# Second attention fed from on-chip q, k and v, and another order of scores within a slot

## The reference

```
x = x + ga * attn0(layernorm(x) * (1 + ca) + sa)     # layer 0: 16 heads of 16, 4096 given keys and values
x = x + gb * ffn0(layernorm(x) * (1 + cb) + sb)      # 8 experts, top 2, bfloat16 products
x = x + ga' * attn1(layernorm(x) * (1 + ca') + sa')  # layer 1: 16 heads of 16, k and v from the same 1024 tokens
x = x + gb' * ffn1(layernorm(x) * (1 + cb') + sb')   # a causal attention with 16 heads of 128, then 16 experts, top 6
```

## Time and profile before

| what | value |
|---|---|
| three timed runs | 2124.57, 2126.62, 2134.29 us; median 2126.62 us |
| profiled execution | 2117.84 us, span of its trace 2116.0 us |
| PE / DVE / ACT / POOL busy | 1746.9 / 1427.0 / 1085.5 / 526.8 us |
| mean granted TensorE clock | 0.889 of full |
| attention 0, first to last second score | about 105 to 771 us |
| attention 1, block begins, first pass begins, last sums taken | 946, 956, 1270 us |
| share of attention 0 and 1 in the page's costliest rows | first pass maxima on DVE 757.7 us, exponentials on ACT 668.8 us |

### The profile page before, as it was taken

The page is one execution under the profiler, slowest core; times in us unless marked ns, Lnnn a source line. Parts: engine busy times, 40 slices in busy tenths (PEclk is TensorE's granted clock), DMA queues, the critical chain, the costliest instruction groups (busy, mean ns, idle before and its releaser), DMA issues. The chain is left out here.

```text
span 2116.0 us, 28258 instructions
## 1 busy us (share of the span) xinstructions
PE 1746.9 (83%) x9835; PEld 1051.8 (50%) x9836; DVE 1427.0 (67%) x1894; ACT 1085.5 (51%) x2169; POOL 526.8 (25%) x541
## 2 busy tenths in 40 slices
PE   3599999999999983445468891599999999859997
PEld 3144343343434323232123331488888888748886
DVE  5589999999999934624346763666666666656665
ACT  1078777777877771222235670345455544424432
POOL 3323432343234101213233311211111111002223
PEclk7599999999999995675768995699999999959998
DMA  3211111111111022133112213100000000023432
GB/s 105 49 50 40 44 53 50 43 43 52 47 48 38 16 90 66 41 119 65 51 49 72 68 66 98 39 14 20 20 8 20 20 12 10 1 52 114 120 106 65
DMA packets 54448, 110.17 MB, mean 52 GB/s; under 512 B 8761, under 2 KB 23097, under 8 KB 52819
## 3 DMA queue, kind: packets, MB, share of 16 engines
q1 hardware_dynamic: 52835, 106.07, 17.3%
q10 hardware_dynamic: 1520, 2.88, 0.5%
HBM read 79.33 MB, written 23.31 MB: 49 GB/s over the span
## 5 line engine op out<-in xcount | busy, mean ns | idle before, releaser
L393 DVE TENSOR_REDUCE a_max_part<-psum 128x1 f32<-128x1024 f32 x640 | 757.7, 1220 | 186.1 <-PE psum L296 180.7
L443 ACT ACTIVATE a_probs<-psum 128x512 f32<-128x512 f32 x1280 | 668.8, 604 | 200.3 <-PE psum L347 198.9
L347 PE MATMUL psum<-a_q_max,a_k_rows 51*128 51x512 f32 x1280 | 456.1, 494 | 8.7 <-ACT a_probs L443 7.3
L347 PEld LDWEIGHTS psum<-a_q_max,a_k_rows 51*128 51x128 f32 x1280 | 183.7, 192 | 406.7 <-ACT a_probs L443 308.8
L336 PE MATMUL psum<-a_probs,a_v_ext 128*32 128x512 f32 x2560 | 359.0, 635 | 0.0
L296 PE MATMUL psum<-a_k_rows,a_q_rows 48*128 48x512 f32 x1280 | 317.0, 449 | 49.3 <-DMA a_q_rows<-q 23.8
L296 PEld LDWEIGHTS psum<-a_k_rows,a_q_rows 48*128 48x128 f32 x1280 | 150.6, 201 | 85.7 <-DVE a_max_part L393 33.5
L168 POOL TENSOR_TENSOR a_k_rows<-a_k_in,a_k_rows 16x2048 fp32r<-16x2048 f32 (+1 forms) x64 | 187.3, 2926 | 4.9
L1518 PE MATMUL psum<-high_t_parts,high_gu 128*128 128x512 f32 x600 | 146.5, 395 | 6.8 <-DVE high_t_parts L1612 6.8
L254 POOL TENSOR_TENSOR a_max_bf<-a_neg_max,a_zeros 128x8 bf16<-128x8 f32 x64 | 14.5, 227 | 488.7 <-issue 470.1
L1223 PE MATMUL psum<-wide_k_t,wide_q_t 128*128 128x512 f32 (+3 forms) x576 | 131.2, 355 | 1.7 <-DVE wide_id_bf L1422 1.7
(11 more groups left out here) (175 smaller groups left out, 2056.4 us busy)
## 6 DMA issues: line engine op xcount, KB each, us to landing
o<-a_o_out SPq DMA_DIRECT2D x64, 256.0 KB, 2.0
a_k_in<-in_k SPq DMA_DIRECT2D x32, 256.0 KB
gu_in<-in_w_gu SPq DMA_DIRECT2D x25, 256.0 KB, 2.9
a_q_rows<-q SPq DMA_DIRECT2D x32, 192.0 KB, 3.5
high_cw<-cw SPq DMA_DIRECT2D x24, 256.0 KB, 3.9
a_k_in<-in_k SPq DMA_DIRECT2D x32, 128.0 KB
a_v_in<-in_v SPq DMA_DIRECT2D x16, 256.0 KB, 12.7
a_q_rows<-q_high SPq DMA_DIRECT2D x64, 64.0 KB, 2.4
```

What stands on the lines that cost most here:

```text
L347: pe.matmul(psum[:, self.bank_of(self.filling(j)), :], k_rows[rows, b, k0:k0 + P], self.q_max[rows, u % 2, :], start=True, stop=True).then ...
L393: dve.tensor_reduce(self.max_part[:, u % 2, c // self.nch, c % self.nch:c % self.nch + 1], psum[:, 2 * (n % 2):2 * (n % 2) + 2, :], AX.XY, ...
L443: act.activation(self.probs[:, p % self.pring, :], psum[:, self.bank_of(self.filling(j)), :], ACT.Exp).then_inc(self.exp_done, 1)
```

## The change

**Attention 1 without DRAM.** `project` for layer 1 makes high and low parts of k as well as of q (`highs`, `lows`), in the order q, k of the first eight heads, then q, k of the others, and leaves v in `v_sb` in SBUF. The tensors q1, k1, v1, their stores and the loads of k and v are gone, and so is `split_keys` in attention 1; `copy_v` reads `v_sb`. The attention's tiles are now there during `project`, whose block clears them on POOL (`prepare`). `load_q` for attention 1 is twelve DMAs a head, SBUF to SBUF: per strip three of q (16 partitions by 1,024) and three of k (16 partitions by 512).

**Who issues, and when.** For head 0, in both attentions, SP issues strip 0 and ACT strip 1. Only heads 0 to 2 are loaded before the first unit; in attention 1 heads 3 to 5 now follow one per unit, and later heads as their buffers come free.

**Clears.** `q_rows`, `max_bf` and `v_ext` are cleared by POOL in the block ahead (`clear`) instead of by DVE at the start of the attention's own block; in attention 0 that is in setup.

**Slot order.** Second score j, pair `one` (strip 1, then 0), second score j+1, the turning of the maxima where the slot has it, pair `two` (strip 0, then 1), second scores j+2 and j+3, products.

The core of the diff:

```diff
+def send_rows(eng, strips, rows, sources, h, per_strip, loaded):
+    at = HD * (h % 8)
+    for n in strips:
+        cols = slice(0, T) if per_strip is None else slice(n * per_strip, (n + 1) * per_strip)
+        for m, src in enumerate(sources):
+            row = STRIP * n + HD * m
+            eng.dma_start(rows[row:row + HD, :].bitcast(F32), src[at:at + HD, h // 8, cols].bitcast(F32)).then_inc(loaded, 16)
...
+    def prepare(self, block):
+        @block.gpsimd
+        def _(pool):
+            pool.memset(self.zeros[:, :], 0.0).then_inc(self.zeros_ready, 1)
+            pool.memset(self.k_rows[:, :, :].bitcast(F32), 1.0).then_inc(self.k_set, 1)
+            self.clear(pool)
...
-            load_q(sp, q_rows[:, 0, :], 0, self.q_loaded[0])
-            for h in range(1, nb):
-                load_q(sp, q_rows[:, h, :], h, self.q_loaded[h])
-            for h in range(1, self.early + 1):
-                sp.wait_ge(self.k_split, 2 * h)
-                self.load_k(sp, h)
-                sp.wait_ge(self.v_ready, h)
-                self.load_v(sp, h)
+            load_q(sp, (0,), q_rows[:, 0, :], k_rows[:, 0, :], 0, self.q_loaded[0])
+            for h in range(1, first_heads):
+                load_q(sp, (0, 1), q_rows[:, h, :], k_rows[:, h, :], h, self.q_loaded[h])
+            got = first_heads
...
-                if half == 1 and h + nb < H:
-                    load_q(sp, q_rows[:, h % nb, :], h + nb, self.q_loaded[h % nb])
+                if got < min(H, nb + (u + 1) // 2):
+                    load_q(sp, (0, 1), q_rows[:, got % nb, :], k_rows[:, got % nb, :], got, self.q_loaded[got % nb])
+                    got += 1
...
                 second_wait(u, j)
-                second_wait(u, j + 1)
                 second_chunk(u, j)
-                second_chunk(u, j + 1)
                 if one < self.chunks:
                     first_wait(one)
-                    first_half(one, 0)
-                    first_half(one, 1).then_inc(self.s1_full, 1)
+                    first_half(one, 1)
+                    first_half(one, 0).then_inc(self.s1_full, 1)
+                second_wait(u, j + 1)
+                second_chunk(u, j + 1)
                 if j + 2 == self.turn_at and u + 1 < us:
                     turn_maxima(u + 1)
-                second_wait(u, j + 2)
-                second_chunk(u, j + 2)
                 if two < self.chunks:
                     first_wait(two)
-                    first_half(two, 1)
-                    first_half(two, 0).then_inc(self.s1_full, 1)
-                second_wait(u, j + 3)
-                second_chunk(u, j + 3)
+                    first_half(two, 0)
+                    first_half(two, 1).then_inc(self.s1_full, 1)
+                for n in (j + 2, j + 3):
+                    second_wait(u, n)
+                    second_chunk(u, n)
...
+            act.wait_ge(self.q_set, 1)
+            if not raw:
+                act.wait_ge(self.k_set, 1)
+            load_q(act, (1,), q_rows[:, 0, :], k_rows[:, 0, :], 0, self.q_loaded[0])
             put_row(0)
...
-                attention = Attention(nc, core, psum, ident, ident_bf, "a1", T // P, 6, k1, v1, o1)
+                attention = Attention(nc, core, psum, ident, ident_bf, "a1", T // P, 6, o1, v_sb=v_sb)
```

More of the change, by code:

```diff
@@ L677, in _, with project @@
             act.wait_ge(taken, 4)
-def project(nc, psum, tag, h_t, w, names, q_high, q_low, q_out=None, k_out=None, v_out=None):
+def project(nc, psum, tag, h_t, w, names, highs, lows, v_sb=None, attention=None):
     with ExitStack() as ctx:
         r = Room(nc, ctx, tag, CLEARED)
-        k_sb = r.sb("k", [P, DC, T]) if k_out is not None else None
-        v_sb = r.sb("v", [P, H, TT, HD]) if v_out is not None else None
-        full, high_done, low_done, k_taken = r.sem("full"), r.sem("high_done"), r.sem("low_done"), r.sem("k_taken")
-        v_full, v_taken, stored = r.sem("v_full"), r.sem("v_taken"), r.sem("stored")
+        full, high_done, low_done = r.sem("full"), r.sem("high_done"), r.sem("low_done")
+        v_full, v_taken = r.sem("v_full"), r.sem("v_taken")
         block = r.block()
-        pieces = [(i, c, half) for i in range(1 if k_out is None else 2) for c in range(DC) for half in range(2)]
-        if q_out is not None:
-            @block.sync
-            def _(sp):
-                heads = P // HD
-                for c in range(DC):
-                    sp.wait_ge(high_done, 2 * c + 2)
-                    sp.wait_ge(low_done, 2 * c + 2)
-                    for at, src in ((0, q_high), (HD, q_low), (2 * HD, q_high)):
-                        sp.dma_start(q_out[heads * c:heads * (c + 1), at:at + HD, :], src[:, c, :].bitcast(F32)).then_inc(stored, 16)
-                for c in range(DC):
-                    sp.wait_ge(k_taken, 2 * c + 2)
-                    sp.dma_start(k_out[c * P:(c + 1) * P, :], k_sb[:, c, :]).then_inc(stored, 16)
-                sp.wait_ge(v_taken, TT)
-                sp.dma_start(v_out.rearrange("h p n -> p h n"),
-                             v_sb[:, :, :, :].rearrange("p h t d -> p h (t d)")).then_inc(stored, 16)
-                sp.wait_ge(stored, 16 * (4 * DC + 1))
+        pieces = [(i, c, half) for c in range(DC) for i in range(len(highs)) for half in range(2)]
+        if attention is not None:
+            attention.prepare(block)
         @block.tensor
@@ L716, in _ @@
                 mm.then_inc(full, 1)
-            if v_out is not None:
+            if v_sb is not None:
                 for t in range(TT):
@@ L728, in _ @@
             for n, (i, c, half) in enumerate(pieces):
[L729 removed]
                 act.wait_ge(full, n + 1)
[L731 to L735 removed]
+                act.activation(highs[i][:, c, half * 512:(half + 1) * 512], psum[:, 4 + n % 4, :], ACT.Copy,
+                               scale=0.25 if i == 0 else 1.0).then_inc(high_done, 1)
+            if v_sb is not None:
                 for t in range(TT):
@@ L1661, in adaln_two_layers, with load_q @@
             with ExitStack() as core:
-                attention = Attention(nc, core, psum, ident, ident_bf, "a0", nk0 // P, 3, i["k0"], i["v0"], o0)
+                attention = Attention(nc, core, psum, ident, ident_bf, "a0", nk0 // P, 3, o0, i["k0"], i["v0"])
                 q_high = core.enter_context(nc.sbuf_tensor("q_high", [P, DC, T], F32R))
                 q_low = core.enter_context(nc.sbuf_tensor("q_low", [P, DC, T], F32R))
-                def load_q(sp, rows, h, loaded):
-                    at = HD * (h % 8)
-                    for n in range(2):
-                        for m, src in enumerate((q_high, q_low, q_high)):
-                            row = STRIP * n + HD * m
-                            sp.dma_start(rows[row:row + HD, :].bitcast(F32), src[at:at + HD, h // 8, :].bitcast(F32)).then_inc(loaded, 16)
+                def load_q(eng, strips, q_rows, k_rows, h, loaded):
+                    send_rows(eng, strips, q_rows, (q_high, q_low, q_high), h, None, loaded)
                 with ExitStack() as front:
@@ L1703, in adaln_two_layers @@
-        with ExitStack() as part:
             o4 = part.enter_context(nc.sbuf_tensor("o4_1", [P, DC, 4, T], F32))
             with ExitStack() as core:
-                attention = Attention(nc, core, psum, ident, ident_bf, "a1", T // P, 6, k1, v1, o1)
-                def load_q(sp, rows, h, loaded):
-                    for n in range(2):
-                        sp.dma_start(rows[STRIP * n:STRIP * n + MROW, :].bitcast(F32), q1[h, :, :]).then_inc(loaded, 16)
+                v_sb = core.enter_context(nc.sbuf_tensor("v_sb", [P, H, TT, HD], F32))
@@ L1712, in adaln_two_layers @@
+                with ExitStack() as front:
+                    wqkv = front.enter_context(nc.sbuf_tensor("wqkv", [P, DC, 3, D], F32))
+                    normalise(nc, psum, "n2", x, ident, False, mod_col[:, 10:12], mod_col[:, 8:10], h_t,
+                              loads=[(wqkv[:, :, :, :].rearrange("p c i n -> p c (i n)"), chunks(i["wqkv1"]))])
+                    project(nc, psum, "p1", h_t, wqkv, 3, (q_high, k_high), (q_low, k_low), v_sb, attention)
                 with nc.Block() as block:
-                    attention.prefetch(block)
@@ L1714, in adaln_two_layers @@
-                    attention.run(block, load_q, 2, o4)
+                    attention.run(block, load_q, 12, o4)
             merge_heads(nc, psum, "m1", 1, o4, o1, den1, i["wproj1"], gates[:, 2, :], x, i["bproj"])
```

82 lines of the change are left out of this document (45 added, 37 removed).

## The result

The changed kernel takes 2006.73 us (median of four runs, 2004.29 to 2010.42) against 2125.6 us for the kernel before (four runs, 2124.02 to 2134.29). The ratio is 0.9434, 95% interval 0.9403 to 0.9466: 5.7% faster. The forecast was 1997 us, range 1971 to 2032.

A forecast was written before the change was run, and what follows sets the result against it. Early attention 1 was held bound by the loop of sums, load, split and maxima. Terms -23.9 - 105.3 + 5 - 1.9 = -126.1 us took 2117.84 to 1991.7, or 2000.5 by the median; forecast between them 1997 us, range 1971 to 2032.

The forecast's parts named there:

- Bound and body: Attention 1: without k load, split and v load, the 28 units after the first fall to 5.68 us each, -105.3 us.
- Slot order, 0: All 320 slots: the new order changes nothing, a slot of attention 0 stays 2.61 us; 0.05 us allowed either way.
- the cycle: Each slot: score j, its latency, exponential j, score j+3, products, next score j set the slot's 2.61 us.
- First pass to first exponential, 14.1: Start of attention 1: this stretch takes 14.1 us instead of 20.8, -6.7 us.
- Projection to first pass, 6.16: Start of attention 1: first pass starts 6.16 us after the projection's last copy, -17.2 us; SP and ACT issue six pieces each.
- issues of over 0.7 us: Sign that the prediction is wrong: SP's DMA issues taking over 0.7 us.
- SP's queue, +5: Attention 1: stores of sums queue behind SP's loads of heads 3 to 8, delaying DVE around unit 6 to 8, about +5 us once.
- Attention 0's start, -1.9: Start of attention 0: SP issues 15 pieces instead of 18 ahead of the k load, which goes 1.9 us earlier.
- the sum made from the median: Whole kernel: the predicted saving taken from the timed runs' median, 8.8 us above the profiled execution, giving 2000.5 us.

The follow-up runs named there:

- the three buffers: Kernel before, still through DRAM with POOL splitting keys, but three buffers instead of one for incoming k and v in attention 1: 2059.47 us, ratio 0.9687.
- the paced loads: Changed kernel with attention 1's heads 3 and on loaded one per two units instead of one per unit: 1994.29 us; a second set 2000.7 us.
- two tests of the cycle: Changed kernel with pair `one` ahead of second score j: 2069.05 us; changed kernel with products between second scores j+2 and j+3: 2029.17 us.

## Why the prediction was right

**Bound and body.** The loop of sums, single-buffered load, split and maxima was the bound of the early units, shown by the three buffers. The unit came down to 5.69 us (forecast 5.68) from unit 2 on; unit 1 took 6.14. The term was -105.3 us, and with the paced loads it measured -104.4.

**Slot order, 0.** Right for the unit of attention 0, shown from both sides: alone the new order left that unit at 21.32 us, and taken out it left the whole ratio at 0.944. A few us in attention 1 of the kernel through DRAM are not excluded. The two tests of the cycle show why: what stands before score j costs its full length, and with the products moved the chain is the same.

**First pass to first exponential, 14.1.** Measured 14.09.

**Projection to first pass, 6.16.** Measured 8.40. The term was mis-sized by 2.2 us: I let ACT's issues run beside SP's for nothing. The rows show them slowing each other, 2.37 and 2.24 us for two pieces each against 1.22, and SP alone costs only 0.8 us more than both. The prediction had named issues of over 0.7 us as a sign of being wrong; these were over 1.1, though most other issues of SP took 0.59. The Trainium skill, "Perfetto Trace Analysis", section on the HWDGE DMA instruction, with descriptor generation locked for one issuer at a time, was nearer to it than I was: by that rule the split gives nothing, by mine 3.8 us, and 0.8 was measured. The trace does not follow the rule to the letter: the twelve issues took 5.4 us on two queues, where twelve after one another take 7.5 us.

**SP's queue, +5.** The mechanism was right, and the place too: DVE waited for stores before the sums of units 6, 7 and 8. The size was half of what this trace shows, 10.1 us by the paced kernel. A load with its store took 7.9 to 9.2 us, mean 8.5, where I had 8.0, and the three waits come to 7.5 us. The rest is a thing the prediction doesn't have: after the waits the granted clock was 0.65 in unit 9 and 0.86 in unit 10, and these two took 1.9 us more than 5.69 each without waiting for any store. In the two traces in which the clock was 1.00 there, the whole cost was 6.9 and 5.1 us, near the forecast.

**Attention 0's start, -1.9.** Partly there. SP issues the k load at 75.38, 11.5 us after the projection's end, where it was 11.85: 0.3 us earlier. But the trace before was the quickest of its kind: in the three others in which SP issues head 0 alone the k load goes 12.7 to 13.0 us after the projection's end, and with the split it goes 11.1 to 11.6. The first sums come at 132.19 against 132.30, in an execution whose projection ended 1.0 us later, so the stretch between is 1.1 us shorter.

**Unlooked-for.** The last three units took 15.05 us instead of 18.17. The clock stayed up there, as busy time by stretch shows, the kernel after and then before:

```profile
1137.00:1153.00 16.00, 13.80 (x81) 3.98 (x73) 2.99 (x6) 11.77 (x23) 0.89 (x4) 1.00 0.24 70
```

```profile
1252.00:1270.00 18.00, 16.02 (x73) 4.39 (x70) 1.90 (x4) 11.04 (x21) 0.89 (x4) 0.75 0.32 108
```

The gap after attention 1 was 12.6 us longer in the profiled execution, and 20.84 us in the next. First exponential to first sums takes 11.92 us against 10.52, and 10.36 to 12.07 in the variants; the two traces differ there in the granted clock, 0.50 against 0.63. The prediction took each stretch over at the clock that the trace before had in it, and in these three places (unit 0, units 9 and 10, the last three units) the clock was another one.

**The number.** 2006.7 against 1997, and against 2000.5 by the sum made from the median. Trace against trace the shortfall is larger, 18.8 us of span, and the table adds it up: 2.6 before attention 1, 2.2 to the first pass, 1.4 to unit 0's sums, 6.0 to unit 28's, 12.6 in the gap, less 3.1 in the last three units and 3.0 after the gap. The 12.6 us are mostly one execution's. That the median came within 10 us of the forecast is in part luck: terms too small for the start and the queue stand against a slower baseline for the forecast and a faster end. Executions of one kernel spread over 6 us and more, so the sum can't be closed further.

## What to carry to other kernels

Before ranking engines by busy time, look at the same loop early and late. Where its period differs by three times, a queue or a single buffer outside it sets the pace, and here more buffers removed it in the first five units, and no transfer in all. When one engine stands in a cycle of a few buffers, look for its links first: here reordering what is no link left the unit as it was, and what was put ahead of a link cost its full length. When a load becomes many small DMAs, multiply the issues by their time and set that against the period of what else must go out on that queue; here pacing the same loads took 7 to 10 us out of the stretch. And when a stretch doesn't come out as forecast, read the granted clock beside the busy time before looking for another wait.

## What the hardware did unexpectedly

Two queues that issue small SBUF to SBUF DMAs at the same time gain 0.8 us of a possible 3.8 over twelve issues, each issue taking about twice its 0.59 us for part of the time. At the end of attention 0, where one kind of matmul runs out and PE is busy 13.1 of 16 us, TensorE's granted clock fell from 1.00 to 0.50 in some executions, and 10.9 us were lost in one unit of 20. With matmuls of no use in the time that PE had free it stayed up in the one trace taken, and the medians were 4 to 11 us lower; that the matmuls are the cause is likely and not shown. At the start of attention 1 PE ran 11.92 us without a pause at 0.50. A store of 256 KB that is issued behind 2 MB of reads on the same queue made DVE wait 7.05 us for it.
